# Prologue of a deformable-convolution and spectral-mixing kernel: one 128-row matmul per bank for the mixing sums, four warming matmuls, filter rows earlier, one inverse-root chain

## What is computed

```python
x = x + _L0_conv_ref(_ln_c(x), offset_w, offset_b, mask_w, mask_b, weight, bn_gamma, bn_beta, bn_mean, bn_var)
scale = bn_gamma / jnp.sqrt(bn_var + BN_EPS)          # inside _L0_conv_ref
```

```python
out = jnp.einsum('btkd,k,kde->bte', U_plus, sigma ** 0.25, Mpp)
out = out + jnp.einsum('btkd,k,kde->bte', U_minus, sigma ** 0.25, Mpm)
t = t + sum_over_branches(weights[i] * pad(_stu(_ln_t(t)[:, :T // (1, 2, 4, 8)[i]], ...)))
```

## Time and profile before

| what | us |
|---|---|
| median of 3 runs | 725.98 |
| lowest and highest | 724.54, 726.33 |
| the profiled execution, its own time | 725.11 |
| its span, first to last instruction | 723.3 |
| PE busy, of 3678 matmul records | 493.3 |
| POOL busy, of 295 instructions | 290.5 |
| DVE busy, of 800 instructions | 314.7 |

### The profile page before, as it was taken

The page is one execution under the profiler, slowest core; times in us unless marked ns, Lnnn a source line. Parts: engine busy times, 40 slices in busy tenths (PEclk is TensorE's granted clock), DMA queues, the critical chain, the costliest instruction groups (busy, mean ns, idle before and its releaser), DMA issues.

```text
span 723.3 us, 9279 instructions
## 1 busy us (share of the span) xinstructions
PE 493.3 (68%) x3678; PEld 279.6 (39%) x3678; DVE 314.7 (44%) x800; ACT 167.6 (23%) x421; POOL 290.5 (40%) x295
## 2 busy tenths in 40 slices
PE   5977429334733983697459944997238636999998
PEld 3543104222522541254025611565125313565566
DVE  6468320749910980197006650079019701843000
ACT  1112003112401420241023300343024102433322
POOL 1157760450774277237710775007732771000000
PEclk9967557756865995699569965999659956999999
DMA  8525346830232133113310332003321331000000
GB/s 170 124 82 157 106 117 215 263 100 0 86 105 73 30 95 102 44 37 97 106 32 2 88 102 81 1 10 94 106 62 30 102 102 37 8 1 2 9 1 8
DMA packets 43763, 54.03 MB, mean 75 GB/s; under 512 B 24664, under 2 KB 34142, under 8 KB 43721
## 3 DMA queue, kind: packets, MB, share of 16 engines
q0 software_dynamic: 13824, 37.77, 18.0%
q1 hardware_dynamic: 23841, 13.42, 6.8%
q10 hardware_dynamic: 6056, 2.26, 1.3%
HBM read 50.12 MB, written 3.30 MB: 74 GB/s over the span
## 4 chain that ended last, share of the span: by engine, by line
PE 53%; issue 18%; another core or an unknown queue 18%; DVE 4%; ACT 4%; DMA 1%; SPq 1%; DVEq 0%
PE bank L891 28%; PE bank L903 7%; PE bank L836 3%; PE bank L762 2%; PE bank L826 2%; ACT u_conv L662 2%; PE bank L743 1%; PE bank L922 1%; PE bank L734 1%; PE bank L795 1%; PE bank L797 1%; DMA filt<-in_L_ffn_phi_dram 1%; PE bank L847 1%; DVE sil L468 1%
## 5 line engine op out<-in xcount | busy, mean ns | idle before, releaser
L269 POOL DMA_INDIRECT G<-corner_table,idx x288 | 287.9, 1000 | 310.0 <-DVE idx L362 191.3
L891 PE MATMUL bank<-filt,u_hi 128*64 128x512 f16 x1280 | 219.3, 405 | 55.8 <-issue 23.5
L662 ACT ACTIVATE u_conv<-bank,f_scale 128x256 f32<-128x256 f32 x256 | 106.0, 470 | 307.3 <-remote 159.6
L891 PE MATMUL bank<-filt,u_lo 128*64 128x512 f16 x640 | 142.0, 402 | 6.7 <-issue 6.2
L891 PEld LDWEIGHTS bank<-filt,u_hi 128*64 128x64 f16 x1280 | 80.3, 113 | 128.5 <-issue 48.0
L459 DVE TENSOR_TENSOR V<-G 128x576 f32<-128x576 f32 x32 | 24.3, 758 | 189.4 <-PE bank L827 111.6
L903 PE MATMUL bank<-u_conv,mixw 128*64 128x256 f32 (+1 forms) x640 | 87.1, 357 | 26.1 <-issue 25.9
L455 DVE TENSOR_TENSOR G<-G,bank 128x2304 f32<-128x2304 f32 x32 | 81.6, 2549 | 0.3
L903 PEld LDWEIGHTS bank<-u_conv,mixw 128*64 128x64 f32 x640 | 48.8, 144 | 50.7 <-issue 38.5
L891 PEld LDWEIGHTS bank<-filt,u_lo 128*64 128x64 f16 x640 | 43.3, 114 | 46.7 <-issue 19.1
L836 PE MATMUL bank<-vT,w_main 128*64 128x128 f32 (+1 forms) x320 | 26.2, 301 | 44.0 <-issue 40.9
(11 more groups left out here) (158 smaller groups left out, 369.8 us busy)
## 6 DMA issues: line engine op xcount, KB each, us to landing
filt<-filter_rows SPq DMA_DIRECT2D x16, 514.0 KB, 7.9
G<-corner_table,idx POOLq DMA_INDIRECT x288
corner_table<-n_uT SPq DMA_DIRECT2D x12, 128.0 KB, 2.8
mixw<-in_x_dram SPq DMA_DIRECT2D x2, 512.0 KB, 6.1
filt<-in_L_ffn_M_phi_plus_dram SPq DMA_DIRECT2D x8, 128.0 KB, 4.3
out_dram<-o_sb ACTq DMA_DIRECT2D x8, 128.0 KB, 1.9
filt<-n_L_ffn_M_phi_minus_dram ACTq DMA_DIRECT2D x4, 128.0 KB, 4.0
corner_table<-n_uT ACTq DMA_DIRECT2D x4, 128.0 KB, 2.8
```

Of the source, the lines that this page charges most:

```text
L269: pool.indirect_dma_start(G[:, k, tap, :], None, corners[bp], bass.IndirectOffsetOnAxis(ap=idx[:, q % 2, k, tap:tap + 1], axis=0)).then_in ...
L662: act.activation(u_conv[:, g % 2, k, b2], conv_ps[b2][:, 2 * P * k:2 * P * k + 2 * P].rearrange("c (p a) -> c p a", p=2), ACT.Copy, scale= ...
L891: last = pe.matmul(conv_ps[b2][C * src:C * src + C, :].rearrange("c (k p a) -> c k p a", k=2, p=2), u[:, NJ * bp + j2, b2, src], h, start= ...
```

## The change

Four things in the prologue, and nothing in the main loop.

- **The sums.** The matrices are laid with the plus ones on partitions 0 to 63 and the minus ones on 64 to 127, and the constant that comes with the identity has two tiles of signs. One matmul of 128 rows per branch and bank takes the place of two of 64 rows: 16 for 32. A diagonal is one DVE instruction per branch (L399) in place of five. The matrices are loaded by 8 transfers in place of 16, one per branch and set. The identity's load is 256 KB in place of 192.
- **The warming matmuls** before the first `turn_normalised` are four, not nine.
- **The filter rows** are made right after `positions` of slots 1 and 3, and SP stores them ahead of the second pair's tables. `weigh(0, 0, 0)` then comes before `normalise_pixels(1)`, `weigh(0, 0, 1)` right behind it, and `positions(1)` and `weights(1)` after both. The memset of `vT` comes earlier.
- **The roots.** One chain of eleven steps over a tile `roots` gives the batch norm's two roots and the first root of sigma; before, these were three chains. The root of the root of sigma stays a chain of its own.

```diff
-WARM_UP = 9
+WARM_UP = 4
-        ident_swap = sb("ident_swap", [P, 3, P])
+        ident_swap = sb("ident_swap", [P, 4, P])
-        fold = ident_swap[:, 2, 0:C]
+        fold, signs = ident_swap[:, 2, 0:C], ident_swap[:, 2:4, :]
+        roots = sb("roots", [P, 3, C + K])
...
-                for kh in range(2):
-                    engine.dma_start(m_raw[C * kh:C * kh + C, r, i, :].rearrange("d (k e) -> d k e", k=8),
-                                     ap(m, (r * K + 8 * kh) * C * C, [[C, C], [C * C, 8], [1, C]])).then_inc(s_mats, 16)
+                engine.dma_start(m_raw[C * i:C * i + C, r, :].rearrange("d (k e) -> d k e", k=K),
+                                 ap(m, r * K * C * C, [[C, C], [C * C, K], [1, C]])).then_inc(s_mats, 16)
...
                 for r in range(BRANCHES):
-                    for v in range(3):
-                        dst = w_diag[:, r, v, :].rearrange("c (h d) -> c h d", h=2)
-                        if v == 0:
-                            last = dve.tensor_scalar(dst, both, br[:, 9, r:r + 1], None, ALU.mult)
-                            continue
-                        for h in range(2):
-                            sign = 1.0 if h == v - 1 else -1.0
-                            last = dve.tensor_scalar(dst[:, h], both[:, h], br[:, 9, r:r + 1], sign, ALU.mult, ALU.mult)
+                    last = dve.tensor_scalar(w_diag[:, r], signs, br[:, 9, r:r + 1], None, ALU.mult)
                 last.then_inc(w_diag_ready, 1)
 
+            def inverse_roots():
+
+                dve.wait_ge(s_bn, 16 * 7)
+                link(dve.tensor_scalar(roots[:, 0, 0:C], roots[:, 0, 0:C], BN_EPS, None, ALU.add))
+                rsqrt(roots[:, 1], roots[:, 0], roots[:, 2])
...
+            filter_rows()
             masks(0)
             weights(0)
+            weigh(0, 0, 0)
+            normalise_pixels(1, (0, 1))
+            weigh(0, 0, 1)
             positions(1)
             weights(1)
-            normalise_pixels(1, (0, 1))
-            weigh(0, 0, 0)
+            inverse_roots()
             main_weights()
-            weigh(0, 0, 1)
-            filter_rows()
...
-                        pe.matmul(bank[b][:], w_diag[rows, r, 0, :], m_raw[rows, r, 0],
-                                  start=(r == 0), stop=False, skip_group_check=True)
-                        pe.matmul(bank[b][:], w_diag[rows, r, 1 + p, :], m_raw[rows, r, 1],
-                                  start=False, stop=(r == BRANCHES - 1), skip_group_check=True).then_inc(mats_summed, 1)
+                        pe.matmul(bank[b][:], w_diag[:, r, p, :], m_raw[:, r, 512 * kh:512 * kh + 512],
+                                  start=(r == 0), stop=(r == BRANCHES - 1), skip_group_check=True).then_inc(mats_summed, 1)
```

More of the change, by code:

```diff
@@ L123, in metaformer_kernel @@
         late = 8 * 2 * HLEN
-        m_raw = filt[:, late:late + 4096].rearrange("d (r m k e) -> d r m (k e)", r=BRANCHES, m=2, k=8)
+        m_raw = filt[:, late:late + 4096].rearrange("d (r k e) -> d r (k e)", r=BRANCHES, k=K)
         n_pad_flat = filt[:, late + 4096:late + 4096 + BP * PH * PW]
@@ L295, in _ @@
             dve.memset(ones[:], 1.0).then_inc(ones_ready, 1)
+            dve.memset(roots[:, 0, 0:C], 1.0).then_inc(roots_set, 1)
             dve.memset(f_rows, 0.0)
@@ L425, in main_weights @@
                 dve.wait_ge(s_w, 16)
[L426 to L428 removed]
+                link(dve.tensor_tensor(bn_col[:, 0:1], bn_col[:, 0:1], roots[0:C, 1, 0:1], ALU.mult))
                 dve.tensor_scalar(w_scaled[:].rearrange("o (t c) -> o t c", t=TAPS),
@@ L549, in _ @@
         def _(act):
-            for i, v in enumerate((sigma, log_weights, gumbel)):
-                dst = sig[:, 0, :] if i == 0 else br[:, i - 1, :]
-                act.dma_start(dst, ap(v, 0, [[0, P], [1, K if i == 0 else BRANCHES]])).then_inc(s_small, 16)
+            for i, v in enumerate((log_weights, gumbel)):
+                act.dma_start(br[:, i, :], ap(v, 0, [[0, P], [1, BRANCHES]])).then_inc(s_small, 16)
             act.dma_start(w_raw, ap(weight, 0, [[C * TAPS, C], [1, C * TAPS]])).then_inc(s_w, 16)
-            for i, v in enumerate((gamma, var)):
-                act.dma_start(bn_col[:, i:i + 1], ap(v, 0, [[1, C], [1, 1]])).then_inc(s_bn, 16)
-            for i, v in enumerate((gamma, beta, mean, var)):
+            act.dma_start(roots[:, 0, C:C + K], ap(sigma, 0, [[0, P], [1, K]])).then_inc(s_bn, 16)
+            act.dma_start(bn_col[:, 0:1], ap(gamma, 0, [[1, C], [1, 1]])).then_inc(s_bn, 16)
+            for i, v in enumerate((gamma, beta, mean)):
                 act.dma_start(bn_row[C:C + 1, i, :], ap(v, 0, [[C, 1], [1, C]])).then_inc(s_bn, 16)
+            act.wait_ge(roots_set, 1)
+            act.dma_start(roots[0:C, 0, 0:1], ap(var, 0, [[1, C], [1, 1]])).then_inc(s_bn, 16)
+            act.dma_start(roots[C:C + 1, 0, 0:C], ap(var, 0, [[C, 1], [1, C]])).then_inc(s_bn, 16)
             for s in (u_copied, *conv_copied):
@@ L733, in keep_warm @@
                 for _ in range(n):
-                    pe.matmul(bank[6][:, 0:3 * P], ident, ident_swap[:].rearrange("s m c -> s (m c)"), start=True, stop=True)
+                    pe.matmul(bank[6][:, 0:3 * P], ident, ident_swap[:, 0:3].rearrange("s m c -> s (m c)"), start=True, stop=True)
             def turn_normalised(bp, b2):
@@ L790, in _ @@
                     for kh in range(2):
-                        rows = slice(C * kh, C * kh + C)
                         b = 2 * p + kh
@@ L979, in constants @@
     first = np.array([k % 2 * IMAGE for k in range(BLK)], np.float32)
-    return {"ident": np.stack([np.eye(P), np.eye(P)[::-1], np.tile(np.eye(C), (2, 2))], 1).astype(np.float32), "grid": grid, "first_row": np.tile(first, (P, 1))}
+    one = np.eye(C)
+    signs = [np.block([[one, one], [h * one, -h * one]]) for h in (1, -1)]
+    return {"ident": np.stack([np.eye(P), np.eye(P)[::-1], *signs], 1).astype(np.float32), "grid": grid, "first_row": np.tile(first, (P, 1))}
 def kernel(**inputs):
```

38 lines of the change are left out of this document (14 added, 24 removed).

## The result

The changed kernel takes 715.83 us (median of 4 runs, 714.2 to 717.95) where the kernel before takes 725.26 (median of 4): a ratio of 0.9879, 95% interval 0.9836 to 0.9922. That is 9.4 us less; the forecast was 714.0, range 704 to 722.5. The profiled execution took 715.25 us, its span is 713.4. Executions of a kernel fall into a fast and a slow group: a ratio with an interval compares the fast ones alone, and of the two kernels with a wait at every slot three runs of four, the profiled one among them, are in the slow group.

What follows compares the result with a forecast made beforehand. While POOL gathers, other engines' instructions were taken to get through slowly, so their number, not length, bounds the prologue. From 725.1, terms of -3.0, -0.5, -7.5 and 0 gave 714.1 us, left at 714; range 704 to 722.5.

Steps and rivals of the forecast that it cites:

- term A: Ahead of the first gather: five warming matmuls fewer save 3.2 us, the larger identity load costs 0.2; -3.0 us.
- The rival of a late clock: First offset convolution: the clock rises later, so its 5 us take 10 and the whole is 719; chance 0.07.
- term B: First run of gathers: 16 DVE instructions less shorten ACT's late copy after the first convolution; -0.5 us, bounds 0 and -3.5.
- term C: Prologue's second run of gathers: fewer instructions let the sums finish early, so second-pair offsets come sooner; -7.5 us, bounds -2.4 and -11.1.
- With a stock of 73 records and some 1 per 1.4 us besides: Mixing sums while POOL gathers: PE gets 87 records through by 67 us, so the sums' 80 are through in time.
- From there the old 129.71 - 113.94 = 15.8 us, less 1.8: After the gathers: old time from second pair's turning to its offsets at DVE, less turning done beforehand; 122.2 for 129.7.
- With the sums out of the way I take 3.4: End of the prologue's second run of gathers: engines are released 3.4 us after the last gather's issue, at 108.2.
- term D: Prologue on DVE: early filter rows and merged root chains fall into time when DVE waits anyway; 0 us.
- DVE caught ahead of the indices, 737: Unit 1's indices come late behind 49 other DVE instructions, POOL stands 20 us, the whole is 737; chance 0.06.
- The second hold opens, 706.5: After the second value contraction: ACT's late copy comes sooner through 12 fewer DVE instructions; another -7.5 us, 706.5; chance 0.13.
- The main loop unchanged at 554.8: Main loop, from its first L891 to the end: stays 554.8 us; differing by more than a few microseconds would show error.

Runs made afterwards that it cites:

- two kernels with a wait at every slot: POOL waits ahead of each slot's nine gathers until the slot ahead has landed: in the changed kernel 590.62 us, in the kernel before 621.14 us.
- second profile of the same kernel: The changed kernel measured again, unaltered, beside other experiments on another chip: ratio 0.9842 of the kernel before.
- tiny matmuls: Changed kernel with one tiny matmul into an unused bank ahead of each of the 16 of the sums: ratio 0.9857 of the kernel before.
- the two parts alone: Kernel before with only four warming matmuls for nine, ratio 0.9932; kernel before with only the merged sums, ratio 0.9911.
- the experiment that gave eleven back: Changed kernel with eleven more small, unused DVE steps at the head of the last root chain: ratio 0.9902 of the kernel before.
- the warming matmuls, on another chip: Changed kernel with four warming matmuls between the second pair's two offset convolutions: 713.09 us beside the changed kernel's 716.84.
- the run of 45 with one wait: Changed kernel where POOL waits, ahead of unit 0's last slot, until PE has convolved the second pair's offsets: ratio 0.9787 of the kernel before.

## Why the prediction was right, and where it was wrong

**Warming matmuls, term A (-3.0).** Right: the first gather came 2.8 us earlier, forecast 3.0. The parts differ a little. The first turn was 3.55 us earlier; the first offset turns then ran at the low clock, 1.87 us for the 1.10 of before. The rival of a late clock did not come: the first convolution took 5 us in every profile with four warming matmuls.

**Diagonals, term B (-0.5).** Inside its bounds: the copy at 38.49 is 1.4 us behind its matmuls, 3.55 before; in the second profile of the same kernel it is 2.6 behind, so the size is not sure. At the sums' start A and B together are 3.7, forecast 3.5.

**The sums, term C (-7.5).** From the sums' start to the offsets at DVE the change gained 5.6 us more, inside the bounds. That the count of instructions matters held up (32 records of tiny matmuls stopped PE earlier). Three steps failed:

- "With a stock of 73 records and some 1 per 1.4 us besides": PE got 186 through, all 64 of the turning and a part of the convolution, where I let 21 of the turning through.
- "From there the old 129.71 - 113.94 = 15.8 us, less 1.8": 14.0 us forecast, and 14.25 measured (106.18 to 120.43), but for another reason. Far more was done beforehand than I had assumed, and I had priced the rest at the clock of before. There the turning stood behind the hold, and the clock was high for all that followed; moved ahead of the hold it left 39 records of convolution at 1.2 GHz, and the offset turns and the values too. Two errors cancelled.
- "With the sums out of the way I take 3.4": PE's pace came back at 106.18, 4.7 us after the last gather of the run at 101.46. These 1.3 us, and a last gather 0.1 us later than forecast, are most of the 1.7 us that the offsets missed.

The Trainium skill ("TensorE: Matmul & The Clock Gate", Part 1: The HAM clock gate) ties the rise of the clock to how busy PE has been. The traces here do not bear that out by busy time alone: in the changed kernel PE was busy for 13.60 of 14.00 us, and the clock stayed at 0.50; with the merged sums alone it was busy for 13.57 of 14.00 us (106 to 120), and the clock rose. What made the difference stays open.

**Filter rows and roots, term D (0).** Right within about 5 us, by the two parts alone.

**DVE caught ahead of the indices, 737.** Did not come: POOL's 45 gathers were unbroken.

**The second hold opens, 706.5 (chance 0.13).** This came, and I had given it little. ACT's copy was 1.0 us late in place of 7.5. The reason that I gave, twelve DVE instructions less, falls with the experiment that gave eleven back. POOL's pause inside those 18 gathers is the likelier one. Where POOL did not stop (0.30 us, its usual gap), in the two experiments on one part alone, the copy was 5.6 and 7.6 us late; where it paused 3.9 to 4.0 us, in four kernels, 1.0 to 2.5 us. In between it is open: after 1.55 us (the tiny matmuls) the copy was 7.1 us late, after 1.53 us (the warming matmuls, on another chip) 2.6.

**The main loop unchanged at 554.8.** It is 557.9, 3.1 us longer; I had named that as a sign of being wrong. The low clock is a possible cause, not a shown one, since single runs of one kernel differ by as much: PE's clock in the first 24 us is 0.80, 0.84 before, with 20 matmul records fewer started ahead of that unit's hold; and where the warming matmuls had brought the clock back, the main loop was 3.0 us shorter.

So the sum of 714 came out by cancelling, and that is luck: 1.7 us less than forecast at the offsets, 2.7 lost on the slow way from there to the second weigh (-9.3 to -6.6), 6.5 gained by the opened hold, 3.1 lost in the main loop. Loss and gain may hang together: it was the slow way to the second weigh that made POOL pause, and the pause is the likelier reason for the opened hold.

## What to carry to other kernels

Where engines idle without a shown releaser for as long as POOL gathers, look at the length of the unbroken run of gathers before looking at the work: nine gathers and a wait for their landing took 18% off the changed kernel, while less and earlier work inside the hold had moved 1%. Count instructions in such a stretch, tiny ones too. And when work is moved ahead of a stall, ask what will wake PE's clock behind it.

## What the runs showed of the hardware that I had not expected

- A long run of indirect gathers holds up the other engines of the core. In the changed kernel PE got 25 records through in 27 us of it, ACT 4 instructions and DVE 13; in the run of 45 with one wait an ACT copy started 35.1 us after its matmuls, with the transfers at a share of 0.35, and 6.4 us after the last gather. The Trainium skill ("SBUF — State Buffer", Who interferes with whom) says that a transfer never contends with a compute engine. That rule is about memory ports, and no run here shows which resource it is; but the engines' starts do depend on the gathers. Each run's time here comes with a span and a clock from its own records, so whether a run without such records has the hold is not shown either.
- It is the pause that clears it: a wait that does not stop POOL changed nothing (0.981), a pause of 2 to 5 us after nine gathers did (0.813), after 18 only partly (0.946). A limit below the few gathers that are under way anyway was not tried.
- PE's clock stayed at 1.2 GHz through the last 10.16 us of convolution with 64 x 32 tiles and the 3.67 us of offset turns behind it, 13.60 of 14.00 us busy. It was high where 128-row turns or warming matmuls stood ahead of the convolution, and where the whole convolution stood behind the hold it rose within it (0.50 up to 116 us, 0.82 over 116 to 120).
